# Moving the node products of a graph layer into its edge loop, and rearranging the node stage

## The chip, the cores and the metric

One core of one Trainium2 chip runs the whole kernel. The metric is the device time of one execution in microseconds (us). Five engines work side by side: TensorE (PE, whose weight loads the profile lists as PEld), VectorE (DVE), ScalarE (ACT), GpSimd (POOL) and SyncE (SP, which issues most transfers).

## The reference

A graph layer over 3125 nodes and 50000 edges sorted by target, followed by a mixture of eight experts, two per node. Both are residual.

```python
x_i, x_j = x[tgt], x[src]                       # x normalised per node, 256 features
h   = relu(concat([x_i, x_j - x_i]) @ W1 + b1)  # 512 hidden
msg = h @ W2 + b2
out = segment_sum(msg, tgt) / (deg + 1e-8)
x = x + out
xn = (layernorm(layernorm(x))) * gamma + beta
top_vals, top_idx = top_k(xn @ Wr + br, 2);  w = softmax(top_vals)
y_e = gelu(xn @ W1[e] + b1[e]) @ W2[e] + b2[e]
x = x + sum over the two chosen e of y_e * w_e
```

The kernel uses that the sum over edges can be taken before the product with W2: it sums the hidden rows of a node first and multiplies the sum.

## The kernel before, in words

Nodes are cut in 25 tiles of 128. The targets are skewed, so tile 0 has 81 blocks of 128 edges and tile 21 has 9; in all 403 blocks are filled of the 408 slots that the loop runs over.

**Preparation.** Every tile is normalised and multiplied by the lower half of W1, and the result `q` goes to memory. DVE works out where each node tile's edges start (`find_tiles`, line 594). It also sets `unsorted`, which sends the kernel into a slow general mode with up to 25 passes where the input does not fit the schedule.

**Edge loop** (lines 958 to 1531), written out as a list of steps, one for each slot. For a slot POOL gathers 128 rows of `q` (L997, 256 KB, a ring of 16 buffers). ACT copies them into a PSUM bank ("seed", L1210). PE adds the target's own part with two products (L1368, L1369). ACT rounds the relu (`h_hi`, L1226), DVE takes the rest (`h_lo`, L1054), and PE adds both into the node tile's sum (L1426, L1427). Five PSUM banks, `z_bank`, are taken in turn by the steps, and seed k waits until DVE is done with step k - 5. PE counts edges for every fourth slot (L1358). Where a node tile is complete, ACT copies its sum to `agg_all` and clears the bank (`close`, L1243 and L1250).

After every fourth slot up to slot 187 there is a "half" step: PE computes half of a tile's own part (`half_product`, L1402, and a filling product over the rest of the bank, L1373) and DVE stores it (L1076, L1098). Three more half steps for W2, after slots 207, 211 and 215, turn it and multiply it with the router's weights. SP reloads x and loads W2 in the loop (L968, L987), between the small loads that DVE's one-hot tiles wait for (L374, L1047).

**Node stage** (lines 1574 on). For each of the 25 tiles PE turns the sum (L1906, four transposes), ACT copies it (L1871), PE multiplies it with W2 and with W2 times the router's weights, 264 columns (L1913, eight instructions), POOL makes the bias (L1855) and adds it to x (L1858). DVE forms the router's part (L1640) and the residual (L1643), then statistics (L1648, L1652). ACT takes the root (L1875), DVE the inverse (L1656) and the negative mean (L1660), and ACT writes the normalised tile (L1880). SP stores x (L1580) and the normalised tile (L1584), 128 KB each, and after each third tile it loads one expert's weights (L1587, L1588, 512 KB each). All of this goes through one queue of SP. The normalised tiles live in a ring of four buffers (`XT_RING`), so that tile t can be written when the store of tile t - 4 has landed.

The expert choice runs in three parts of 16 DVE steps (`decide`): tiles 0 to 9 and 10 to 17 are interleaved with the tiles, 18 to 24 come last. When the last part is done (`s_diff`), PE computes ranks (L1926, L1927) after `AWAKE[0]` filling products (L365), then come `AWAKE[1]` more, then 100 products that list each expert's tokens (L1934), and from this list POOL starts the token gathers (L1571). The expert stage has 56 slots and is bound by PE.

Of the kernel before, what the change touches and what calls it, by code (L numbers as in the profile page):

```python
# [28 lines left out]
P = 128  # L29
EPS = 1e-5  # L30
# [6 lines left out]
AWAKE = (32, 32, 14, 6)  # L37
# [4 lines left out]
NODE_TILES = 25  # L42
HALF_PERIOD = 4
W2_GAP = 5
# [5 lines left out]
XT_RING = 4  # L50

# [28 lines left out]
def build(nc, x, src, dst, g_w1, g_b1, g_w2, g_b2, gamma, beta, wr, br, f_w1, f_b1, f_w2, f_b2, out):  # L80
# [16 lines left out]
    BATCH = 5  # L97
    assert NT == NODE_TILES and NT % 2 == 1 and 2 * H == 1024 and D == 256 and f_w1.shape[2] == H and f_w2.shape[2] == D
# [18 lines left out]
    with ctx:  # L117
# [57 lines left out]
        unsorted = sb("unsorted", [P, 1], F32, edge_ctx)  # L175
        tsort = sb("tsort", [P, SC], F32, edge_ctx)
# [13 lines left out]
        soonest = whole("soonest", [P, 1], F32, a_ctx)  # L190
        too_short = whole("too_short", [P, 32], F32, a_ctx)
# [78 lines left out]
        bias_in = sb("bias_in", [P, 2, D], F32, c_ctx)  # L270
# [89 lines left out]
        s_rel = [sem(f"s_rel{k}") for k in range(REL_RING)]  # L360

# [21 lines left out]
        with nc.Block(no_gpsimd_drain=True) as block:  # L383
# [45 lines left out]
            def _(pool):  # L429
# [21 lines left out]
                for k in range(2):  # L451
                    pool.memset(pad_i[0:1, k, :], -k).then_inc(s_const, 1)
                pool.memset(tile_hot[:].bitcast(F32), 0.0).then_inc(s_bc, 1)
# [32 lines left out]
            def _(dve):  # L486
# [107 lines left out]
                def find_tiles():  # L594
# [4 lines left out]
                    then(dve.tensor_tensor(too_soon[:, 0:NT], first_ok[:, 0:NT], base[0][:, 0:NT], ALU.is_gt))  # L599
                    now()  # L600
                    then(dve.tensor_reduce(soonest[:, :], too_soon[:, READY:NT + 1], AX.X, ALU.max))
# [10 lines left out]
                    now()  # L612

# [219 lines left out]
        s_high = sem("s_high")  # L833
        s_xback = sem("s_xback")
# [5 lines left out]
        P_HALVES = PARTS * (NT - READY)  # L840
        HALVES = P_HALVES + KD + 1
        w2_turned = [x_all[:, NT - 5 + 2 * k:NT - 3 + 2 * k, :].rearrange("p a d -> p (a d)") for k in range(KD)]
        steps = []
        for j in range(NS):
            steps.append(("slot", j))
            if half_after(j) is not None and half_after(j) < HALVES:
                steps.append(("half", half_after(j)))
        step_at = {what: k for k, what in enumerate(steps)}

        def step_no(slot0, j):  # L850

            return step_at["slot", slot0 + j] if isinstance(slot0, int) else slot0 + (j + HALVES)

        rounded = [what for what in steps if what[0] == "slot" or what[1] >= P_HALVES]
# [6 lines left out]
        def z_of(slot0, j):  # L861

            return z_bank[step_no(slot0, j) % FIRST_RING if isinstance(slot0, int) else (j + NS_ALL + HALVES) % Z_RING]
# [1279 lines left out]
```

## Time and profile before

| | |
|---|---|
| median of 3 runs | 902.34 us (899.70 to 903.33) |
| the profiled execution | 904.58 us, span 902.8 us |
| busy share of the span | PE 94%, PEld 75%, DVE 71%, ACT 71%, POOL 67% |
| edge loop, first gather to last sum | 64.5 to about 593 us |
| node stage, from its first transposes to the ranks | 595.3 to 660.7 us |
| lists of tokens | 660.7 to 681.9 us |
| expert stage | from there to the end |

Engines and lines are named as in the text above. A matmul's end is modelled and overlaps the next one, so the distance from start to start is what one costs where PE is full.

### The profile page before, as it was taken

What the parts mean: (1) busy time and instruction counts of PE and PEld (TensorE: products, weight loads), DVE (VectorE), ACT (ScalarE), POOL (GpSimd) and SP (SyncE); (2) the same over time, 40 slices, a digit from 0 to 9 for tenths busy, and PEclk for the clock granted to TensorE, in tenths of its full rate; (3) what the DMA queues carried; (4) which work ended last, traced back from release to release, by engine and by line L of the source; (5) the groups of instructions that cost most, each with busy time, mean ns of one, the idle gap of its engine ahead of it and who ended that gap; (6) DMA issues with size and microseconds to landing.
All of it is one profiled execution on the core that took longest, in us unless ns stands there. A gap on an engine that the chain in (4) does not pass through costs nothing. (4 is left out here: it accounts for less than half of the span.)

```text
span 902.8 us, 16689 instructions
## 1 busy us (share of the span) xinstructions
PE 850.4 (94%) x4164; PEld 675.2 (75%) x4165; DVE 642.3 (71%) x1762; ACT 641.3 (71%) x1398; POOL 602.9 (67%) x615
## 2 busy tenths in 40 slices
PE   9988999999999889988989888889999999999997
PEld 5446888877887668655656666668888999999996
DVE  6847898988998778877768778646894454455553
ACT  4426888888898789988989899835554555555553
POOL 2327777777777777777777777559304677776864
PEclk9998999999999989999999999999999999999999
DMA  8557877787787887887777787729852344443544
GB/s 254 174 160 225 258 240 240 240 246 244 241 238 241 240 265 233 240 248 242 241 238 238 228 240 228 208 54 279 267 134 55 60 72 72 77 78 61 83 67 49
DMA packets 90974, 169.24 MB, mean 187 GB/s; under 512 B 17608, under 2 KB 56910, under 8 KB 90840
## 3 DMA queue, kind: packets, MB, share of 16 engines
q0 software_dynamic: 43696, 122.35, 49.8%
q1 hardware_dynamic: 46232, 44.79, 16.6%
q10 hardware_dynamic: 944, 0.92, 0.4%
q8 instruction: 42, 0.69, 0.3%
q14 instruction: 60, 0.49, 0.2%
HBM read 146.98 MB, written 21.43 MB: 187 GB/s over the span
## 5 line engine op out<-in xcount | busy, mean ns | idle before, releaser
L997 POOL DMA_INDIRECT gath<-q_rows,idx_t x408 | 391.5, 960 | 137.1 <-issue 88.8
L1054 DVE SCALAR_TENSOR_TENSOR h_lo<-bank,h_hi 128x512 fp32r<-128x512 f32 x366 | 244.6, 685 | 58.5 <-ACT h_hi L1226 55.6
L1226 ACT ACTIVATE h_hi<-bank 128x512 fp32r<-128x512 f32 x366 | 216.0, 595 | 35.4 <-PE bank L1369 18.9
L1210 ACT ACTIVATE bank<-gath 128x512 f32<-128x512 f32 x366 | 219.8, 603 | 22.5 <-DMA gath<-q_rows,idx_t 17.1
L1368 PE MATMUL bank<-p_hi,ohT 128*128 x366 | 154.6, 422 | 29.9 <-ACT bank L1210 22.9
L1426 PE MATMUL agg_ps<-h_hi,oh 128*128 128x512 f32 x408 | 164.7, 404 | 2.7 <-DVE h_lo L1054 2.7
L1427 PE MATMUL agg_ps<-h_lo,oh 128*128 128x512 f32 x408 | 164.0, 402 | 0.0
L1369 PE MATMUL bank<-p_lo,ohT 128*128 x366 | 146.1, 399 | 0.0
L1368 PEld LDWEIGHTS bank<-p_hi,ohT 128*128 128x128 f32 x366 | 70.2, 192 | 74.1 <-issue 60.0
L1989 POOL DMA_INDIRECT out<-y_out,sca_i x56 | 91.7, 1637 | 40.3 <-issue 16.5
L2093 PE MATMUL bank<-tokT,fw_now 128*128 128x128 f32 x896 | 109.3, 275 | 0.8 <-ACT tokT L2049 0.8
L2059 ACT ACTIVATE actT<-bank,b1T 128x128 f32<-128x128 f32 x224 | 64.2, 368 | 61.4 <-PE bank L2093 61.4
L2105 PE MATMUL agg_ps<-fw,actT 128*128 x448 | 105.9, 380 | 0.1
L2093 PEld LDWEIGHTS bank<-tokT,fw_now 128*128 128x128 f32 x896 | 104.5, 192 | 1.0 <-DVE fw_now L2012 1.0
L1571 POOL DMA_INDIRECT agg_all<-xm_rows,gat_i x56 | 60.9, 1088 | 65.5 <-DVEq L1811 40.6
L1426 PEld LDWEIGHTS agg_ps<-h_hi,oh 128*128 128x128 f32 x408 | 78.5, 192 | 23.7 <-issue 4.6
L1040 DVE TENSOR_SCALAR oh<-iota_row,rel_t 128x128 fp32r<-128x128 f32 x408 | 91.5, 302 | 2.4 <-issue 2.4
L2032 DVE TENSOR_TENSOR y_out<-agg_ps,b2f 128x256 f32<-128x256 f32 x56 | 23.8, 425 | 95.7 <-PE agg_ps L2105 77.7
L1427 PEld LDWEIGHTS agg_ps<-h_lo,oh 128*128 128x128 f32 x408 | 78.6, 193 | 15.2
L2105 PEld LDWEIGHTS agg_ps<-fw,actT 128*128 128x128 f32 x448 | 80.9, 190 | 9.0 <-issue 0.3
L1369 PEld LDWEIGHTS bank<-p_lo,ohT 128*128 128x128 f32 x366 | 70.6, 193 | 13.0
L2049 ACT ACTIVATE tokT<-bank,gain_T 128x128 f32<-128x128 f32 x112 | 45.2, 454 | 38.9 <-PE bank L2083 38.9
(279 smaller groups left out, 1117.6 us busy)
## 6 DMA issues: line engine op xcount, KB each, us to landing
rows_sb<-rel_blocks SPq DMA_DIRECT2D x102, 128.0 KB, 4.3
fw<-in_L_ffn_W SPq DMA_DIRECT2D x16, 512.0 KB, 5.2
gath<-q_rows,idx_t POOLq DMA_INDIRECT x408, 4.3
q_rows<-q_buf SPq DMA_DIRECT2D x25, 256.0 KB, 2.8
out<-x_all SPq DMA_DIRECT2D x28, 128.0 KB, 4.0
x_all<-in_x SPq DMA_DIRECT2D x25, 128.0 KB, 2.4
xm_rows<-xt SPq DMA_DIRECT2D x25, 128.0 KB, 3.6
x_all<-in_x SPq DMA_DIRECT2D x2, 640.0 KB, 10.8
```

Of the source, the lines that this page charges most:

```text
L997: pool.indirect_dma_start(out=gath[:, j % RING, :], out_offset=None, in_=q_rows[:, :], in_offset=bass.IndirectOffsetOnAxis(ap=idx_t[:, j:j ...
L1040: ins = dve.tensor_scalar(oh[:, q % 4, k, :], iota_row[:], rel_t[:, bass.ds(local + k, 1)], None, ALU.is_equal)
L1054: dve.scalar_tensor_tensor(out=h_lo[:, j % LO_RING, :], in0=z_of(slot0, j), scalar=0.0, in1=h_hi[:, j % HI_RING, :].bitcast(F32), op0=ALU. ...
L1210: actv.activation(z_of(slot0, j), gath[:, j % RING, :], ACT.Copy).then_inc(s_seed, 1)
L1226: actv.activation(h_hi[:, j % HI_RING, :], z_of(slot0, j), ACT.Relu).then_inc(s_hi, 1)
L1368: pe.matmul(z, w, p_hi[:, tile, :], start=False, stop=True, skip_group_check=True)
L1369: pe.matmul(z, w, p_lo[:, tile, :], start=False, stop=True, skip_group_check=True).then_inc(s_exp, 1)
L1426: pe.matmul(agg_ps[:, par, :], w, h_hi[:, j % HI_RING, :], **more)
L1427: pe.matmul(agg_ps[:, par, :], w, h_lo[:, j % LO_RING, :], **more).then_inc(s_sum, 1)
L1989: pool.indirect_dma_start(out=out[:, :], out_offset=bass.IndirectOffsetOnAxis(ap=sca_i[:, i:i + 1], axis=0), in_=y_out[:, i % OUTS, :], in ...
L2093: ins = pe.matmul(bank[i % 2][:, h * P:(h + 1) * P], fw1_now[:, i % 2, k, h * P:(h + 1) * P], tokT[:, i % 2, k * P:(k + 1) * P], start=(k ...
L2105: ins = pe.matmul(agg_ps[:, i % 2, 0:D], actT[:, i % 2, k * P:(k + 1) * P], fw2[:, experts[i], k, :], start=(k == 0), stop=(k == KH - 1))
```

## The change

- 22 node tiles (`IN_LOOP`) are turned and multiplied inside the edge loop: a "turn" step after slot 211 + 9t and a "product" step after slot 217 + 9t. Each takes a bank of the ring. DVE stores the results with a predicated copy; the predicate `in_order` is false only in the slow general mode. The turned sum replaces `p_lo` of that tile, and the product replaces the sum in `agg_all`.
- Three tiles remain in the node stage, each with a bank of its own.
- The half steps for W2 come after slots 199, 203 and 207.
- Preparation compares the end of each tile with the slot by which it has to be closed, and sets `unsorted` where it is late.
- The bias is made by ACT, in a ring of four, up to nine tiles ahead; POOL only adds.
- The 22 tiles' router parts are formed by two operations. Their residual reads the product from SBUF. Root, inverse and negative mean are taken for groups of 3 or 4 tiles (`ROOTS`).
- The stores of the normalised tiles come six tiles behind those of x. `AWAKE[0]` goes from 32 to 112.

```diff
-AWAKE = (32, 32, 14, 6)
+AWAKE = (112, 32, 14, 6)
+IN_LOOP, NODE_AT, NODE_EVERY, PRODUCT_AFTER = 22, 211, 9, 6
-W2_GAP = 5
+W2_GAP = 2
+BIASES, BIAS_AHEAD = 4, 9
+        for kind, at in (("turn", NODE_AT), ("product", NODE_AT + PRODUCT_AFTER)):
+            if j >= at and (j - at) % NODE_EVERY == 0 and (j - at) // NODE_EVERY < IN_LOOP:
+                steps.append((kind, (j - at) // NODE_EVERY))
...
+    then(dve.tensor_tensor(too_late[:, 0:IN_LOOP], base[0][:, 1:IN_LOOP + 1], last_ok[:, 0:IN_LOOP], ALU.is_gt))
+    then(dve.tensor_reduce(latest[:, :], too_late[:, 0:IN_LOOP], AX.X, ALU.max))
+    then(dve.tensor_tensor(unsorted[:], unsorted[:], latest[:, :], ALU.max))
+    then(dve.tensor_scalar(in_order[:], unsorted[:], 0.0, None, ALU.is_equal))
...
+                def keep_node(kind, t):
+                    full = z_bank[step_at[kind, t] % FIRST_RING]
+                    if kind == "turn":
+                        dve.wait_ge(s_node_ps, 2 * t + 1)
+                        dve.copy_predicated(aggT_of(t), in_order[:].to_broadcast([P, H]), full).then_inc(s_lo, 1)
+                    else:
+                        dve.wait_ge(s_node_ps, 2 * t + 2)
+                        dve.copy_predicated(node_sum(t), in_order[:].to_broadcast([P, D + NEXP]), full[:, 0:D + NEXP]).then_inc(s_lo, 1)
...
+                def turn_node(t):
+                    at = step_at["turn", t]
+                    wait_after(pe, s_lo, at - FIRST_RING)
+                    wait_after(pe, s_seed, max(j for what, j in steps[:at] if what == "slot"))
+                    for h in range(KH):
+                        ins = pe.matmul(z_bank[at % FIRST_RING][:, h * P:(h + 1) * P], agg_all[:, t, h * P:(h + 1) * P], ident[:],
+                                        start=(h == 0), stop=True, is_transpose=True, skip_group_check=True)
+                    ins.then_inc(s_node_ps, 1)
+                def node_product(t):
+                    wait_after(pe, s_lo, max(at - FIRST_RING, step_at["turn", t]))
+                    for k in range(KH):
+                        pe.matmul(full[:, 0:D + NEXP], aggT_of(t)[:, k * P:(k + 1) * P], w2g[:, k, :],
+                                  start=(k == 0), stop=(k == KH - 1), skip_group_check=True)
+                    rest(full, D + NEXP).then_inc(s_node_ps, 1)
...
+        ROOTS = (0, 3, 6, 10, 14, 18, 22, NT)
+        late_bank = [agg_ps[:, 0, :], agg_ps[:, 1, :], bank7[:]]
                 for t in range(NT):
                     store_x1(t)
-                    if t:
-                        store_xt(t - 1)
+                    if t >= XT_LAG:                  # XT_LAG = 6
+                        store_xt(t - XT_LAG)
                     if t % 3 == 2 and t // 3 < NEXP:
                         load_expert(t // 3)
...
                 def residual(t):
-                    dve.wait_ge(s_gnn, t + 1)
-                    dve.scalar_tensor_tensor(out=logit[:, t, :], in0=agg_ps[:, t % 2, D:D + NEXP], ...)
+                    y = agg_all[:, t, :]
+                    if t >= IN_LOOP:
+                        y = late_bank[t - IN_LOOP]
+                        ...
                     dve.wait_ge(s_res, t + 1)
-                    dve.scalar_tensor_tensor(out=x_all[:, t, :], in0=agg_ps[:, t % 2, 0:D], scalar=rdeg[:, t:t + 1],
+                    dve.scalar_tensor_tensor(out=x_all[:, t, :], in0=y[:, 0:D], scalar=rdeg[:, t:t + 1],
                                              in1=x_all[:, t, :], op0=ALU.mult, op1=ALU.add).then_inc(s_x1, 1)
...
-                for i in range(NT + 1):
+                for i in range(NT + 4):
                     if i < NT:
                         residual(i)
+                    for b in range(len(ROOTS) - 1):
+                        if i == ROOTS[b + 1] + 2:
+                            invert(b)
                     if 0 <= i - 1 < NT:
-                        invert(i - 1)
+                        statistics(i - 1)
...
-                        pool.tensor_scalar(bias_in[:, t % 2, :], b2g, degr[:, t:t + 1], None, ALU.mult).then_inc(s_bias_in, 1)
+                def bias(t):
+                        wait_count(actv, s_res, t + 1 - BIASES)
+                        actv.activation(bias_in[:, t % BIASES, :], b2g, ACT.Copy, scale=degr[:, t:t + 1]).then_inc(s_bias_in, 1)
...
+                for b in range(len(ROOTS) - 1):
+                    root(b)
+                    for t in range(ROOTS[b], ROOTS[b + 1]):
+                        bias(t + BIAS_AHEAD)
+                        normalise(t)
```

## Rows read from the trace of the kernel before

**Rows 1.** Busy time of the engines in three stretches (PE, PEld, DVE, ACT, POOL, clock, DMA share, GB/s):

```profile
200.00:240.00 40.00, 39.71 (x178) 32.30 (x177) 36.20 (x93) 35.17 (x67) 30.24 (x33) 1.00 0.79 243
440.00:480.00 40.00, 34.17 (x131) 24.45 (x131) 30.43 (x72) 35.54 (x69) 30.54 (x32) 0.96 0.79 235
620.00:640.00 20.00, 19.98 (x105) 16.65 (x104) 16.02 (x67) 10.93 (x26) 18.88 (x24) 1.00 0.94 276
```

**Rows 2.** The gathers' line: duration min/median/max, first and last start:

```profile
L997 POOL DMA_INDIRECT gath<-q_rows,idx_t x408: 945/949/1206, 64.5 to 579.2; - x136
```

**Rows 3.** Gathers (L997) from 60 us to a time; count in brackets:

```profile
60.00:340.00 280.00, 209.01 (x219) 0.98 0.79 240
60.00:560.00 500.00, 376.10 (x392) 0.98 0.79 239
```

**Rows 4.** The same for the sums of the slots (L1427; PE and PEld):

```profile
60.00:340.00 280.00, 82.09 (x206) 39.22 (x206) 0.98 0.79 240
60.00:420.00 360.00, 108.28 (x273) 51.81 (x273) 0.98 0.79 240
60.00:560.00 500.00, 152.60 (x383) 73.22 (x383) 0.98 0.79 239
```

**Rows 5.** PE in time order around one half step (start, length, line):

```profile
201.41 1.03 PE L1402 MATMUL deg_ps<-w_wide,x_all 128*128 128x256 f32 x4
202.08 0.46 PE L1373 MATMUL deg_ps<-zero_r 128*128 128x256 f32 x1
202.38 0.39 PE L1358 MATMUL deg_ps<-oh,group_hot 128*102 128x512 f32 x1
```

**Rows 6.** PE in time order, one tile of the node stage:

```profile
626.45 0.60 PE L1906 MATMUL bank<-ident,agg_all 128*128 128x128 f32 x4
626.89 1.95 PE L1913 MATMUL agg_ps<-w_wide,aggT 128*128 128x264 f32 x8
628.67 0.60 PE L1906 MATMUL bank<-ident,agg_all 128*128 128x128 f32 x4
```

**Rows 7.** Waits from 300 to 330 us, the longest of DVE:

```profile
DVE ohT L1047 <- DMA rows_sb<-rel_blocks: 5.7, 1, 5.7
```

**Rows 8.** PE's granted clock in two stretches there (busy, clock, DMA share, GB/s):

```profile
317.00:318.00 1.00, 0.71 (x2) 0.64 1.01 340
...
324.00:325.00 1.00, 1.00 (x5) 0.95 0.57 107
```

**Rows 9.** The node stage's first transposes and SP's first store:

```profile
595.25 1.07 PE L1906 MATMUL bank<-ident,agg_all 128*128 128x128 f32 x8 [0.43 <-PEq L958]
...
599.69 2.17 SPq L1580 DMA_DIRECT2D out<-x_all  x2
```

**Rows 10.** DVE in time order, one tile of the node stage:

```profile
651.72 0.47 DVE L1643 SCALAR_TENSOR_TENSOR x_all<-agg_ps,rdeg,x_all 128x256 f32<-128x256 f32 x1
652.11 0.15 DVE L1656 RECIPROCAL rstd<-std 128x1 f32<-128x1 f32 x1
652.22 0.43 DVE L1648 BATCH_NORM_STATS2 stats<-x_all 128x6 f32<-128x256 f32 x1
...
652.78 0.19 DVE L1706 TENSOR_TENSOR score<-score,top 128x64 f32<-128x64 f32 x1
```

**Rows 11.** A POOL addition and a small DVE operation beside it:

```profile
601.85 0.73 POOL L1858 TENSOR_TENSOR x_all<-x_all,bias_in 128x256 f32<-128x256 f32 x1
601.87 0.72 DVE L1660 SCALAR_TENSOR_TENSOR nmr<-mv,rstd 128x1 f32<-128x1 f32 x1
```

**Rows 12.** DMA in a full stretch of the node stage (clock, share, GB/s):

```profile
629.00:632.00 3.00, 1.00 1.07 373
```

**Rows 13.** End of the choice: filling products, last part's first step, ranks' weight loads:

```profile
653.33 7.24 PEld L365 LDWEIGHTS deg_ps<-ident_r 128*128 128x128 f32 x32
...
656.02 0.17 DVE L1669 TENSOR_TENSOR top<-mv 128x7 f32<-128x7 f32 x1
...
660.68 0.34 PEld L1926 LDWEIGHTS bank<-pick_e,ones_mat 128*128 128x128 f32 x2
```

More of the change, by code:

```diff
@@ L97, in build, with closed_before @@
     BATCH = 5
+    P_HALVES = PARTS * (NT - READY)
+    HALVES = P_HALVES + KD + 1
+    steps = []
+    for j in range(NS):
+        steps.append(("slot", j))
+        if half_after(j) is not None and half_after(j) < HALVES:
+            steps.append(("half", half_after(j)))
+        for kind, at in (("turn", NODE_AT), ("product", NODE_AT + PRODUCT_AFTER)):
+            if j >= at and (j - at) % NODE_EVERY == 0 and (j - at) // NODE_EVERY < IN_LOOP:
+                steps.append((kind, (j - at) // NODE_EVERY))
+    step_at = {what: k for k, what in enumerate(steps)}
+    EXTRA = len(steps) - NS
+    def closed_before(t):
+        at = step_at["turn", t]
+        seeded = max(k for k in range(at) if steps[k][0] == "slot") - FIRST_SEED_AHEAD
+        return max(j for j in range(GROUP - 1, NS, GROUP) if step_at["slot", j] < seeded) + 1
+    LAST_OK = min(closed_before(t) - NODE_EVERY * t for t in range(IN_LOOP))
     assert NT == NODE_TILES and NT % 2 == 1 and 2 * H == 1024 and D == 256 and f_w1.shape[2] == H and f_w2.shape[2] == D
@@ L838, in build @@
         z_bank = [bank[0][:], bank[1][:], bank7[:], deg_ps[:, 1, :], bank[2][:]]
-        P_HALVES = PARTS * (NT - READY)
-        HALVES = P_HALVES + KD + 1
         w2_turned = [x_all[:, NT - 5 + 2 * k:NT - 3 + 2 * k, :].rearrange("p a d -> p (a d)") for k in range(KD)]
[L843 to L848, printed above, removed]
         def step_no(slot0, j):
-            return step_at["slot", slot0 + j] if isinstance(slot0, int) else slot0 + (j + HALVES)
-        rounded = [what for what in steps if what[0] == "slot" or what[1] >= P_HALVES]
+            return step_at["slot", slot0 + j] if isinstance(slot0, int) else slot0 + (j + EXTRA)
+        rounded = [what for what in steps if what[0] == "slot" or what[0] == "half" and what[1] >= P_HALVES]
         hi_at = {what: k for k, what in enumerate(rounded)}
@@ L1292, in fill_first @@
                                 high_half(j)
-                            else:
+                            elif kind == "slot":
                                 relu_hi(0, j)
@@ L1301, in first @@
                         fill_first(k)
[L1302 to L1304 removed]
+                        if kind == "slot":
+                            close_group(j, vals)
                     def fill(slot0, j, last):
@@ L1502, in first @@
                             sum_edges(0, j, known[j], known[(j, j + GROUP - 2)[j % GROUP]] if j % GROUP < 2 else None)
-                        if k + HALF_AHEAD < len(steps) and steps[k + HALF_AHEAD][0] == "half":
-                            half_product(steps[k + HALF_AHEAD][1])
+                        ahead, m = steps[k + HALF_AHEAD] if k + HALF_AHEAD < len(steps) else ("none", 0)
+                        if ahead == "half":
+                            half_product(m)
+                        if ahead == "turn":
+                            turn_node(m)
+                        if ahead == "product":
+                            node_product(m)
                         if kind == "slot" and j % GROUP == 0:
@@ L1918, in _ @@
                 pe.wait_ge(s_w2g, 16)
-                for i in range(1, NT + 1):
-                    if i < NT:
-                        turn_agg(i)
-                    product(i - 1)
+                for r in range(1, NT - IN_LOOP + 1):
+                    if r < NT - IN_LOOP:
+                        turn_agg(r)
+                    product(r - 1)
                 stay_awake(pe, AWAKE[0])
```

160 lines of the change are left out of this document (104 added, 56 removed).

## The prediction, made before the changed kernel was run

> **What bounds the kernel now.** The chain of waits ends at once in the last transfer and says nothing, so I read the busy time by stretch first, then the waits around each change, then the order in time.
>
> In the edge loop PE is busy for 39.7 of 40 us while the half steps run and for 34.2 of 40 later, ACT for 35.5 [rows 1]. POOL's 30 of 40 looks idle, but POOL sets the pace: its 408 gathers go from 64.5 to 579.2 us, so one starts each 514.7 / 407 = 1.265 us [rows 2], or 173 in 220 us between 340 and 560, 1.272 us [rows 3]. Nine slots take 11.4 us. How far the sums lie behind the gathers says whether the rest keeps up: 219 - 206 = 13 slots at 340 us, 392 - 383 = 9 at 560 us [rows 3, 4]. The lag of 13 comes from the load of W2, which held up a small load of DVE's for 5.7 us [rows 7]; PE then ran at half clock (1.2 of 2.4 GHz) from about 317.6 to 324 us [rows 8]. Afterwards the sums made 67 slots in 80 us, 1.19 us each [rows 4]. So spare capacity repaid four slots, 4 x 1.27 = 5.1 us. Nine slots cost the machine 10.7 us and the pace allows 11.4.
>
> In the node stage PE is full: 2.22 us from one tile's transposes to the next [rows 6], and 25 x 2.22 = 55.5 us. POOL is at 18.9 of 20 us there and the DMA engines at 0.94 [rows 1]. This second number matters below. From the stage's start at 595.3 us (T) to the rank products at 660.7 us it is 65.4 us [rows 9, 13].
>
> **The edge loop after the change.** A product over 512 columns costs PE 7.24 / 32 = 0.226 us [rows 13]; I take 0.23. Nine slots hold 36 of them and 2.25 counts: 38.25 x 0.23 = 8.8 us. The change adds per nine slots the transposes, 626.45 to 626.89, 0.44 us, and the product, 626.89 to 628.67, 1.78 us [rows 6]. The filling product over 248 columns shows as 202.08 to 202.38, 0.30 us [rows 5]; part of that belongs to the product before it, since four of 256 columns cannot cost 0.67 us if eight of 264 cost 1.78. So 0.1 to 0.3 us. Sum: 11.1 to 11.3 us against 11.4. PE just fits, but the slack that repaid the four slots is gone. I charge the 5.1 us in full. PE's remaining slack could repay up to 22 x 0.3 = 6 us; against it stands that a block of 1.9 us on PE delays the sum for which ACT waits at every fourth slot. I let these cancel: **+5 us**, with +0 and +25 as ends (the latter under the rivals).
>
> DVE gets a predicated copy of 512 columns and one of 264 per nine slots, an operation that no row shows. The nearest are residuals of 256 columns at 0.39 us from start to start [rows 10], so 1.2 us for both; a second pass would double it, and a copy for which half is enough would cost 0.6. DVE is busy 30.4 of 40 us [rows 1], 8.7 of 11.4, and ends between 9.3 and 11.1. I take 1.2 and no cost: it has 1.5 us of cover left. With the high end the cover is gone, and ACT's seeds, which wait for DVE five steps back, would come late (in the rivals). No step gains a wait of its own: a turn waits for seeds that the expansion before it needs anyway, a product for a copy six slots back, and both for the bank like any step. Moving the W2 half steps eight to twelve slots forward moves 3 us of PE work into the recovery and costs nothing else, as W2 is loaded at the same place.
>
> Preparation gains four small DVE operations, under 0.25 us each by the small ones of [rows 10]. The gathers start behind the stores of q, not behind this table, so I count nothing; without that cover it is 1 us.
>
> **The node stage after the change.** PE needs 3 x 2.22 = 6.7 us and drops out. Four candidates are left, each counted from T.
>
> *DVE.* An iteration between 651.72 and 652.78 takes 1.06 us, of which the inverse is 0.11 (652.11 to 652.22) and I take the same for the negative mean: 0.84 remains for residual and statistics [rows 10]. 25 x 0.84 = 21 us. Seven groups of inverse and mean: 7 x 0.35 = 2.5. Start after degrees, router part and its two new operations: 3.3 (T to the first residual, 3.9 now, less the wait for a product). Choice, parts one and two: the last part's 16 steps and three more run from 656.02 to 660.68, 4.7 us [rows 13], so 4.3 each without the three; 8.6 for two and 4.7 for the last. Together 40 us.
>
> *POOL against DVE.* An operation on 128 x 1 values took 0.72 us instead of 0.14 and ended within 0.01 us of a POOL addition that had started 0.02 us earlier: 601.87 + 0.72 = 602.59, 601.85 + 0.73 = 602.58 [rows 11]. Both read two operands from SBUF. Today's residual reads one from PSUM and is 0.47 us beside POOL's work. In 22 tiles it now reads the product from SBUF. POOL's 25 additions need 25 x 0.73 = 18 us, inside DVE's first half, so some 15 residuals meet one and wait 0.36 us on average: +5 us, with 0 and 22 x 0.73 = 16 as ends. DVE's path is then 45 us.
>
> The Trainium skill, "SBUF — State Buffer", section "Specifications (TRN2)", states this as an exclusive lock on the port pair of VectorE and GpSimd, held for a whole instruction, for a DVE operation with two SBUF inputs against a GpSimd one that reads SBUF. It speaks against moving the product to SBUF, and the trace agrees with 0.72 against 0.14 us [rows 11].
>
> *The transfers.* They were hidden behind PE's 55 us; now they are not. SP's one queue holds x (25 tiles of 0.131 MB), normalised tiles (the same) and experts (8 of 1.05 MB). The last group's root is behind ACT's normalising of tile 21, which needs the buffer of tile 17, whose store is queued behind 24 tiles of x, 17 others and 7 experts: 24 x 0.131 + 18 x 0.131 + 7 x 1.05 = 12.85 MB. The nearest row for a full machine is 373 GB/s at a share of 1.07, or 349 per unit of share [rows 12]; the mean of the stage, 276 at 0.94 [rows 1], gives 294. I take 349, as the stretch that was filled without gaps: 36.8 us. SP's first store is at T + 4.4 [rows 9], and the engines fill only with the first expert, 1.2 us lost: the store lands at T + 42.4. Then 0.6 to normalise, 0.3 root, 0.5 inverse and mean, 4.7 last part, 0.3 in semaphores: ranks at **T + 48.8**. With 294 GB/s it is T + 56.
>
> *ACT* has 25 biases and 25 normalised tiles of 256 columns; even at 0.5 us each, like a DVE operation of that width [rows 10], that is 25 us, and POOL has 20. Both lie beside DVE.
>
> The later one decides: T + 48.8 instead of T + 65.4, **-16.6 us**.
>
> By the Trainium skill, "DMA: Bandwidth & Descriptors", section "Specifications", the fabric carries 435 GB/s and HBM 358 per core; at 435 the store would land at T + 35 and DVE would decide. That is the second rival; no row moves that much over 3 us.
>
> **PE's clock.** PE's three tiles and its 112 filling products end at T + 9 + 112 x 0.226 = T + 34.5; the ranks come at T + 49. In the loop the clock fell to half behind idle time and stayed there for about 6.4 us, 317.6 to 324 [rows 8]. So the ranks and some 12 of the next 32 filling products cost twice: 12 x 0.226 = 2.7 us less a little that DVE's own path hides. **+2.5 us** (0 to 5). The other queued transfers (3.6 MB, ten us) and the tags behind them end before the token lists do, 21 us after the ranks.
>
> **Sum.** 5 - 16.6 + 2.5 = -9.1 us. Profiled time 904.6 becomes 895.5; this execution lay 2.2 us above the median, so the forecast is **893 us**.
>
> **Rivals.**
>
> 1. *The transfers don't bind* (chance 0.22). For: loads alone reach 373 GB/s. Then DVE's 45 us decides, PE is idle for 10 us less, and the sum is 5 - 20.4 + 1 = -14: 888; if the port costs nothing, 883.
>
> 2. *The loop loses more than the stage gains* (0.22, the one with the other sign). Place: PE and ACT at slots 217 to 406. ACT may wait for each of the 22 products because it closes a group every fourth slot and is busy 35.5 of 40 us [rows 1]; the predicated copy at its high end adds to the same path. Price: the 1.1 us by which one product block exceeds a half step's 0.97 us [rows 5], which was hidden, each time: 22 x 1.1 = 24. With -14 behind it that is +10 plus nothing repaid: 912 to 915. It decides from 0.65 us per product upwards (22 x 0.65 = 14). Against: during the half steps PE was at 39.7 of 40 us and the pace held [rows 1].
>
> 3. *Transfers at 294 GB/s* (0.14): 5 - 9.4 + 3 = -1.4: 901.
>
> 4. *The general mode* (0.01): a tile that ends too late for its slot sets `unsorted`, and all is run in 25 passes. With the block counts of this input the nearest of the 22 tiles ends eight slots before its limit; so this is nearly excluded. It would multiply the loop.
>
> **How the numbers follow.** Forecast 0.41. The measurement tells 0.5%, 4.5 us, from no change: faster is below 897.8 us. Forecast and first rival lie below it nearly whole (0.58), and of the others 0.06. The third lies inside, with the edge of the second and the weak end of the forecast: 0.20. Slower: 0.16. The range reaches from the first rival with a free port (0 in the loop, 881) to the second one's beginning, 906.
>
> **What would show it.** Right: L1427's count stays 12 or more slots behind L997 to 560 us and the last sum comes 4 to 6 us later; POOL's pace is unchanged; SP's stores of the normalised tiles take over 8 us to land, ACT waits for them, and the ranks start 47 to 51 us after the stage; residuals have two lengths, near 0.47 and up to 1.2 us; L365 behind the ranks takes longer than 7.3 us. Wrong: a lag of nine slots (the loop cost nothing), or ACT idle before L1226 in each nine slots (rival 2); ranks at T + 45 with stores landing in 4 us (rival 1).

## The result, and where the time went

The changed kernel takes 914.86 us (median of 6 runs, 912.52 to 916.28) against 902.42 us for the kernel before (6 runs, 899.70 to 904.93): ratio 1.0137, 95% interval 1.0118 to 1.0156. It is slower by 1.4%; the forecast was 893 us, in a range of 881 to 906. The profiled execution took 915.1 us and has a span of 913.4, 10.6 more than the 902.8 of before.

Four marks split these 10.6 us. The node stage starts (T) with VectorE's copy of the degrees, at 595.2 us before and at 614.3 now. The rank products' weight load, the first product of the token lists and VectorE's conversion of the list follow. The marks of the changed kernel (first and last start at the end of each row):

```profile
L1728 DVE COPY deg<-deg_ps x1: 185/185/185, 614.3 to 614.3; 128x25 f32<-128x25 f32 x1
...
L2050 PEld LDWEIGHTS bank<-pick_e,ones_mat x2: 286/310/333, 669.4 to 669.5; 128*128 128x128 f32 x2
...
L2058 PE MATMUL bank<-agg_all x100: 214/275/275, 679.9 to 690.9; 128*128 128x56 f32 x100
...
L1926 DVE TENSOR_SCALAR gat_i<-bank x1: 216/216/216, 691.2 to 691.2; 128x56 int32<-128x56 f32 x1
```

| stretch | before | after | difference | forecast |
|---|---|---|---|---|
| up to T | 595.2 | 614.3 | +19.1 | +5 |
| T to the ranks | 65.4 | 55.0 | -10.4 | -16.6 |
| ranks to the first list product | 8.8 | 10.5 | +1.7 | +2.5 |
| from there to the end | 233.3 | 233.5 | +0.2 | 0 |

**The edge loop.** GpSimd's gathers last started at 579.2 us [rows 2], and now ten us later:

```profile
L1034 POOL DMA_INDIRECT gath<-q_rows,idx_t x408: 944/947/1214, 64.6 to 589.3; - x136
```

The number of gathers (first two rows) and of sums (last three) from 60 us on, in brackets, answers to [rows 3, 4]:

```profile
60.00:340.00 280.00, 208.92 (x219) 0.98 0.80 240
60.00:560.00 500.00, 368.41 (x387) 0.98 0.78 235
...
60.00:340.00 280.00, 81.94 (x206) 39.39 (x206) 0.98 0.80 240
60.00:420.00 360.00, 105.07 (x265) 50.49 (x265) 0.98 0.80 240
60.00:560.00 500.00, 145.14 (x367) 69.70 (x367) 0.98 0.78 235
```

At 340 us both kernels stand alike, 219 gathers and 206 sums. Then 161 sums follow in 220 us instead of 177: 1.366 us a slot, 12.3 us for nine, where before it was 1.243. The lag of the sums grows from 13 to 20 slots. That is all it can be: a gather waits for a seed to free one of 16 buffers, and at 560 us there are 387 gathers against 371 seeds, with the sums four slots behind the seeds. So the gathers are held back too, 168 instead of 173. The seeds (L1268):

```profile
60.00:560.00 500.00, 219.77 (x371) 0.98 0.78 235
```

The waits of that stretch (340 to 580 us; total, times, longest) say who held them:

```profile
POOL gath L1034 <- ACT bank L1268: 26.5, 59, 3.1
DVE h_lo L1091 <- ACT h_hi L1284: 23.6, 35, 2.3
DVE ohT L1084 <- PE bank L1426: 22.0, 18, 2.3
...
ACT h_hi L1284 <- PE bank L1426: 16.6, 25, 1.3
ACT h_hi L1284 <- PE deg_ps L1426: 7.5, 7, 3.0
...
DVE ohT L1084 <- PE deg_ps L1426: 5.8, 6, 2.2
```

The same waits before (340 to 560 us):

```profile
POOL gath L997 <- ACT bank L1210: 12.8, 42, 0.3
DVE ohT L1047 <- PE bank L1369: 2.3, 5, 0.7
ACT h_hi L1226 <- PE bank L1369: 1.4, 7, 0.3
```

ScalarE and VectorE now wait for TensorE's expansions (L1426), 24.1 and 27.8 us, and GpSimd for ScalarE's seeds, up to 3.1 us at a time instead of 0.3. The busy times (PE, PEld, DVE, ACT, POOL, then clock, DMA share, GB/s) answer to the second line of [rows 1]:

```profile
440.00:480.00 40.00, 37.90 (x170) 29.16 (x169) 30.76 (x73) 34.65 (x67) 28.75 (x31) 1.00 0.75 230
```

TensorE went from 34.2 to 37.9 of 40 us (and its weight loads from 24.5 to 29.2); VectorE is busy for 30.8 us instead of 30.4, ScalarE and GpSimd for less than before. A node tile's product and its filling product, in order of time (start, length):

```profile
606.56 1.94 PE L1489 MATMUL bank<-w_wide,p_lo 128*128 128x264 f32 x8
608.14 0.46 PE L1430 MATMUL bank<-zero_r 128*128 128x248 f32 x1
608.45 0.40 PE L1520 MATMUL agg_ps<-h_hi,oh 128*128 128x512 f32 x1
```

It is 1.58 us and 0.31, where I had 1.78 and 0.1 to 0.3.

**The node stage.** The end of the path to the ranks, ScalarE first, then VectorE (in brackets the idle time before, and what ended it):

```profile
662.07 1.98 ACT L1993 ACTIVATE xt<-x_all,nmr,rstd 128x256 f32<-128x256 f32 x3 [2.87 <-DMA xm_rows<-xt]
663.96 0.28 ACT L1988 ACTIVATE std<-mv,eps_col 128x3 f32<-128x3 f32 x1
...
664.35 0.18 DVE L1770 RECIPROCAL rstd<-std 128x3 f32<-128x3 f32 x1 [3.64 <-ACT std L1988]
```

This is the chain of the forecast: a store of normalised rows lands at 662.1 us, T + 47.8, three tiles are normalised, the last group's root follows, and VectorE, idle for 3.6 us, makes the last choice. In the stage ScalarE waits 21.6 us for such stores:

```profile
ACT xt L1993 <- DMA xm_rows<-xt: 21.6, 7, 4.6
```

The DMA engines in two stretches of it (columns as in [rows 1]), where [rows 12] had 373 GB/s:

```profile
624.00:628.00 4.00, 4.00 (x19) 3.32 (x18) 3.97 (x16) 3.34 (x9) 4.00 (x6) 1.00 1.07 383
...
648.00:652.00 4.00, 0.35 (x2) 0.00 (x0) 0.77 (x5) 1.40 (x4) 0.49 (x2) 1.00 1.03 276
```

Both are full, and move 383 and 276 GB/s. TensorE, idle from 648 us, is granted half its clock when the ranks come: 0.53 as the mean of 652 to 674 us.

```profile
652.00:674.00 22.00, 4.64 (x10) 0.53 0.80 247
```

### The profile page after: what moved, and what is told of

Its sections match the earlier page's. It is cut to its first block and busy times, and to the rows that moved or that the text cites. A ratio compares the mean times of both kernels' runs of the same rounds, so it can differ in the third digit from the quotient of the medians.

```text
span 913.4 us, 16847 instructions
## 1 busy us (share of the span) xinstructions
PE 857.6 (94%) x4266; PEld 690.6 (76%) x4267; DVE 656.5 (72%) x1754; ACT 638.6 (70%) x1383; POOL 578.7 (63%) x591
## 5 line engine op out<-in xcount | busy, mean ns | idle before, releaser
L1091 DVE SCALAR_TENSOR_TENSOR h_lo<-bank,h_hi 128x512 fp32r<-128x512 f32 x363 | 239.5, 681 | 37.8 <-ACT h_hi L1284 35.7
L1284 ACT ACTIVATE h_hi<-bank 128x512 fp32r<-128x512 f32 x363 | 213.4, 595 | 46.4 <-PE bank L1426 32.5
L1268 ACT ACTIVATE bank<-gath 128x512 f32<-128x512 f32 x363 | 215.7, 601 | 21.8 <-DMA gath<-q_rows,idx_t 10.7
L1425 PE MATMUL bank<-p_hi,ohT 128*128 x363 | 149.9, 413 | 15.9 <-ACT bank L1268 12.4
L1520 PE MATMUL agg_ps<-h_hi,oh 128*128 128x512 f32 x408 | 161.3, 395 | 0.1
L1521 PE MATMUL agg_ps<-h_lo,oh 128*128 128x512 f32 x408 | 161.2, 395 | 0.0
L1426 PE MATMUL bank<-p_lo,ohT 128*128 x363 | 143.5, 395 | 0.0
L2113 POOL DMA_INDIRECT out<-y_out,sca_i x56 | 92.0, 1643 | 41.7 <-issue 16.5
L1084 DVE TENSOR_SCALAR ohT<-rows_sb,slot_no 128x512 fp32r<-128x512 bf16 x102 | 53.6, 526 | 44.6 <-PE bank L1426 34.2
L1426 PEld LDWEIGHTS bank<-p_lo,ohT 128*128 128x128 f32 x363 | 68.9, 190 | 12.2
## 6 DMA issues: line engine op xcount, KB each, us to landing
x_all<-in_x SPq DMA_DIRECT2D x2, 640.0 KB, 10.8
```

Source lines behind the costliest of these rows:

```text
L1091: dve.scalar_tensor_tensor(out=h_lo[:, j % LO_RING, :], in0=z_of(slot0, j), scalar=0.0, in1=h_hi[:, j % HI_RING, :].bitcast(F32), op0=ALU. ...
L1268: actv.activation(z_of(slot0, j), gath[:, j % RING, :], ACT.Copy).then_inc(s_seed, 1)
L1284: actv.activation(h_hi[:, j % HI_RING, :], z_of(slot0, j), ACT.Relu).then_inc(s_hi, 1)
L1425: pe.matmul(z, w, p_hi[:, tile, :], start=False, stop=True, skip_group_check=True)
L1426: pe.matmul(z, w, p_lo[:, tile, :], start=False, stop=True, skip_group_check=True).then_inc(s_exp, 1)
L1520: pe.matmul(agg_ps[:, par, :], w, h_hi[:, j % HI_RING, :], **more)
```

## The experiments

T and the ranks' start are read as above in each, from one profiled execution. Three kernels with the same edge loop (the changed one and the two below that move weights) have T at 614.3, 613.3 and 614.5 us; so I read a difference of 2 us, and no less.

**A first group on a disturbed chip.** Four kernels ran where even the kernel before took 1041.37 us, with stalls of 2 to 5 us on all engines all through the loop: without the product 1041.74 us, with predicated copies of 8 columns 1046.41, with both kinds of step empty 1048.80, and with the product in two pieces 1054.82. Nothing is concluded from them. Two of their questions were asked again. The two that were not leave most of the results unstored. The edit of the first, for the turned sum; the product's copy is cut in the same way:

```
-  dve.copy_predicated(aggT_of(t), in_order[:].to_broadcast([P, H]), full)
+  dve.copy_predicated(aggT_of(t)[:, 0:8], in_order[:].to_broadcast([P, 8]), full[:, 0:8])
...
```

> The changed kernel with both predicated copies cut to 8 columns (the turned sums and the products are not stored, apart from 8 columns). VectorE loses about 0.9 us of work per nine slots. Theory (PE's block): the node stage starts at 610 to 614 us. Rival (VectorE's copies): 596 to 601 us.

The other one has the small copies, and of turn and product only the filling product.

> The changed kernel with its 44 further steps left in the ring of banks but nearly empty: PE issues one filling product over a few columns in each, VectorE copies 8 columns (nothing is turned or multiplied). Theory (PE's block): the node stage starts at 595 to 597 us, as before the change. Rival (a step of the ring costs by itself, because a seed waits for VectorE five steps back and five steps now hold fewer slots): 603 to 610 us.

**Without the product.** The product's four matmuls per node tile are left out and its filling product stays, so the node sums are not multiplied by W2.

```
-  for k in range(KH):
-      pe.matmul(full[:, 0:D + NEXP], aggT_of(t)[:, k * P:(k + 1) * P], w2g[:, k, :], ...)
   rest(full, D + NEXP).then_inc(s_node_ps, 1)
```

> The product's eight instructions left out in each of the 22 product steps, once more. Theory (PE's block): the node stage starts at 596 to 599 us. Rival (VectorE's copies): above 610. Rival (further steps in the ring): above 608.

898.17 us (before on that chip 902.66), T at 597.4:

```profile
L1725 DVE COPY deg<-deg_ps x1: 184/184/184, 597.4 to 597.4; 128x25 f32<-128x25 f32 x1
...
440.00:480.00 40.00, 36.02 (x152) 27.34 (x153) 33.06 (x76) 35.77 (x69) 30.25 (x33) 0.96 0.81 244
```

So 16.9 of the 19.1 us come with the product. Transposes, filling products, both predicated copies and the 44 ring steps, all still there, cost 2.2. Whether copies or steps cost more beside the product than without it was not run on an undisturbed chip.

**The product in two pieces**, in two successive slots: the same work, half the block that sums and expansions wait behind.

```
-  for k in range(KH):
+  for k in range(piece * (KH // PIECES), (piece + 1) * (KH // PIECES)):
...
-  if ahead == "product":
-      node_product(m)
+  for piece in range(PIECES):
+      later = k + HALF_AHEAD - piece
+      if later < len(steps) and steps[later][0] == "product":
+          node_product(steps[later][1], piece)
```

> The whole computation of the changed kernel, a node tile's product issued in two pieces one step apart, once more, because in the first job every kernel, the one before the change too (1041 us), ran with stalls of 2 to 5 us on all engines all through the loop. Theory (ScalarE waits out the length of PE's block): the node stage starts at 602 to 608 us against 614.3, total 905 to 909. Rival (PE has too much work): 612 to 616 us, total 914.

912.23 us, T at 612.6. Halving the block brings 1.7 us, no more than can be read here, where half of 19 was expected. The block's length was the mechanism of my second rival, and it falls; the amount of work stands.

**The order on VectorE.** The transposed one-hot, whose waits for TensorE are new, is built behind the low part.

```
-  if j % GROUP == 2 and j // GROUP + 2 < NG:
-      build_ohT(j // GROUP + 2)
   split_lo(0, j)
+  if j % GROUP == 2 and j // GROUP + 2 < NG:
+      build_ohT(j // GROUP + 2)
```

> The changed kernel, but VectorE builds the next transposed one-hot after the low part of its slot instead of before it. In the changed kernel VectorE waits 28 us there for TensorE's expansions (2.3 us in the kernel before), with the low part that TensorE's sums want queued behind. If this order makes the loop slower, the node stage starts at least 6 us earlier than 614.3 us and the time falls to about 908. If TensorE is simply full, that wait is only where it shows: the node stage starts within 1.5 us of 614.3 and the time is 913 to 915.

911.88 us, T at 611.4. The waits there fall from 27.8 to 6.5 us, and T by 2.9: between the two answers, nearer to the second. Most of a wait of 28 us was a place where the loss shows, not its cause.

**Two and three of the four matmuls**, `range(KH // 2)` and `range(KH - 1)` in the product, whose sums are then incomplete.

> The changed kernel with two of the four matmuls of each of the 22 products left out (its output is not the reference's). With all four the node stage starts at 614.3 us, with none at 597.4. If every microsecond of the product counts once TensorE has no slack, the start lies half way, 605 to 607, and the time is about 906. If there is slack that the first half still fits into (my forecast's picture with a smaller margin), the start is below 601 and the time about 901.

> The changed kernel with one of the four matmuls of each of the 22 products left out (its output is not the reference's). The node stage started at 597.4 us without the product, at 600.6 with two of the matmuls and at 614.3 with all four. A bound that is crossed, after which each further matmul costs its whole time on TensorE (22 x 0.31 = 6.8 us), puts the start with three at 607 to 608. A cost that only the fourth brings would leave it at 601 to 602.

902.73 us and T at 600.6 with two, 904.77 and 604.3 with three. The gathers and sums of the one with two, then of the one with three (the last start, and the counts to 560 us):

```profile
L1034 POOL DMA_INDIRECT gath<-q_rows,idx_t x408: 946/947/1196, 65.0 to 578.0; - x136
...
60.00:560.00 500.00, 375.41 (x393) 0.99 0.80 240
...
60.00:560.00 500.00, 148.13 (x377) 71.27 (x377) 0.99 0.80 240
```

```profile
L1034 POOL DMA_INDIRECT gath<-q_rows,idx_t x408: 946/947/1202, 64.3 to 579.7; - x136
...
60.00:560.00 500.00, 376.29 (x393) 0.99 0.80 239
...
60.00:560.00 500.00, 147.42 (x374) 70.85 (x374) 0.99 0.80 239
```

| matmuls | T | step | last gather | lag at 560 us | PE busy, 440 to 480 us |
|---|---|---|---|---|---|
| none | 597.4 | | 579.5 | 392 - 380 = 12 | 36.0 |
| two | 600.6 | +3.2 | 578.0 | 16 | 36.7 |
| three | 604.3 | +3.7 | 579.7 | 19 | 37.5 |
| four | 614.3 | +10.0 | 589.3 | 387 - 367 = 20 | 37.9 |

One matmul is two records, a quarter of 1.58 us, so 22 x 0.395 = 8.7 us of TensorE's time over the loop. (The 0.31 in my expectation was the filling product's.) The first two, 17.4 us of work, cost 3.2 us together, the third 3.7 and the fourth 10.0, by T. My 607 to 608 for three was too late, and 601 to 602 too early.

T overstates the difference between the third and the fourth. At 300 us, before the first turned tile, the run with three already stood at 179 sums, the one with two at 177 and the one with four at 178, and a slot is worth 1.27 us. The sums of 340 to 560 us alone, without, then with two, three and four matmuls:

```profile
340.00:560.00 220.00, 69.98 (x176) 33.51 (x176) 0.98 0.80 238
340.00:560.00 220.00, 67.65 (x173) 32.54 (x173) 1.00 0.80 239
340.00:560.00 220.00, 65.84 (x168) 31.54 (x168) 1.00 0.81 237
340.00:560.00 220.00, 63.19 (x161) 30.31 (x161) 0.99 0.76 229
```

The first two matmuls cost 3 sums together, the third 5, the fourth 7. One matmul is 19 x 0.395 = 7.5 us of work in that stretch, 5.9 slots. So the first two are mostly hidden, and from the third on each costs about its own time, within the slot or so by which such counts vary (the two kernels that move weights have 162). In the forecast's own prices nine slots hold 10.3, 10.7 and 11.1 us of work with two, three and four, and take 11.4 (the gathers' pace), 11.8 and 12.3. With three and four that is 91 and 90%: as far as this estimate goes, TensorE's limit in this stretch, which the run with two matmuls just meets.

With up to three matmuls the gathers keep their pace and only the lag grows, which is paid once, at the end. With four the lag is at its limit and a late sum delays a gather: of the 19.1 us, 10.1 are the last gather's delay (579.2 to 589.3) and 9.0 the longer lag.

**Weights last.** Of the changed kernel, all 16 loads of experts' weights go behind the last store of normalised rows on SP's queue.

```
-  if t % 3 == 2 and t // 3 < NEXP:
-      load_expert(t // 3)
...
   for t in range(NT - XT_LAG, NT):
       store_xt(t)
+  for e in range(NEXP):
+      load_expert(e)
```

> The changed kernel with the 16 loads of the experts' weights (8.4 MB) issued after the last store of normalised rows instead of between the stores. If transfers hold the node stage, the stores of rows land in 2 to 3 us, ScalarE's 21.6 us of waits for them go below 5, and the ranks come 45 to 48 us after the stage starts instead of 55: 905 to 908 in all. If something else holds it (VectorE's statistics beside GpSimd's additions), the ranks stay at 53 to 55 us and the time at 913 to 915. A cost that could eat the gain: weights that land after the token lists are ready, which would show as TensorE waiting for expert weights in the block after.

912.71 us (4 runs; ratio to before 1.0108, 1.0072 to 1.0144), T at 613.3, ranks at 657.5: 44.2 us instead of 55.0, with 1.9 us instead of 5.4 for a store to land. So transfers held the stage, as forecast, and VectorE's 45 us come out behind them. The end moved by only 2.5 us (span 910.9), for another reason than I had listed: the tags' store is queued behind the weights on SP.

```profile
666.84 1.82 SPq L1691 DMA_DIRECT2D fw<-in_L_ffn_W  x1
...
669.38 2.72 SPq L1691 DMA_DIRECT2D fw<-in_L_ffn_W  x1
...
679.92 0.47 SPq L1708 DMA_DIRECT2D xm_rows<-tags  x1
```

```profile
POOL agg_all L1673 <- DMA xm_rows<-tags: 43.0, 1, 43.0
```

With a full queue even the issuing of one load takes up to 2.7 us, the tags leave at 679.9 us (675.5 as changed), and GpSimd waits for them with the first token gather, which starts at 688.4, 9 us behind the list that was ready at 679.3.

**Half the weights behind the tags.** Four experts between the stores as changed, the other four right behind the tags' store.

```
-  if t % 3 == 2 and t // 3 < NEXP:
+  if t % 3 == 2 and t // 3 < NEXP // 2:
...
   sp.dma_start(xm_rows...[:, :, D:], tags[:, :, :]).then_inc(s_tags, 16)
+  for e in range(NEXP // 2, NEXP):
+      load_expert(e)
```

> The changed kernel with the weights of four experts (4.2 MB) loaded between the stores as before, and those of the other four issued right after the store of the tags. With all eight moved behind the last store of rows the ranks came 44.2 us after the stage began instead of 55.0, but the store of the tags queued behind them. If half the bytes leave transfers enough room and the tags are no longer behind weights, the ranks come at 44 to 47 us and most of the gain reaches the end: 904 to 907. If the weights that come later are missed by the block after them, the ranks still come early and the time stays at 911 to 914.

907.96 us (6 runs; ratio to before 1.0071, 1.0047 to 1.0094), T at 614.5, ranks at 662.2, T + 47.7:

```profile
L2052 PEld LDWEIGHTS bank<-pick_e,ones_mat x2: 288/312/337, 662.2 to 662.4; 128*128 128x128 f32 x2
```

```profile
ACT xt L1995 <- DMA xm_rows<-xt: 8.2, 3, 4.3
```

Of the 7.2 us won at the ranks 6.9 reach the median (about 6 by the ratios, as the kernel before was 1.8 us faster on this chip); tags leave at 665.4 and the first token gather at 685.0. Now the node stage takes 17.7 us less than before, and what is left of the loss is the loop's.

**Fewer tiles in the loop.** IN_LOOP 8 every 24 slots, and 10 every 19, the rest after the loop; their products go through the three banks in a ring, so that product r waits for VectorE's residual r - 3. `AWAKE[0]` is 24, and with ten tiles 28 filling matmuls stand where TensorE would wait for the first bank.

```
-  IN_LOOP, NODE_AT, NODE_EVERY, PRODUCT_AFTER = 22, 211, 9, 6
+  IN_LOOP, NODE_AT, NODE_EVERY, PRODUCT_AFTER = 8, 211, 24, 6
...
+  if r > 2:
+      pe.wait_ge(s_x1, IN_LOOP + r - 2)
```

> Eight node tiles in the loop, one every 24 slots, and 17 after it, through three PSUM banks used in a ring. TensorE needs 2.6 us a tile in the stage of before, so 17 take 44 us, less than the 55 us of the stage. If each product costs the loop its own 0.8 us, the stage starts at 597.5 + 8 x 0.8 = 604; if the loop catches up between products 24 slots apart, at 598 to 600. The ranks come 54 to 55 us later either way, since transfers set that, and the time is 904 or 899 to 900. If TensorE's tiles after all bind the new stage (the rival), ranks come 60 us or more after its start and nothing is won over 905.

> Ten node tiles in the loop, one every 19 slots, 15 after it, with 28 filling matmuls where TensorE would idle for a free bank (it idled 6.6 us there with eight in the loop, and its clock fell to 0.7), and the experts' weights as in g1. The loop should lose 2 to 3 us against the kernel before (stage at 598 to 600), the ranks should come 47 to 50 us after it (TensorE's 15 tiles at 2.6 us and the wait for a bank set that), and the time 890 to 896. If the weights' late arrival costs what the ranks gain, it is 900 or more.

> As g2, but with the experts' weights where the change has them. If transfers hold the stage, its ranks come 54 to 57 us after the start and the time is 898 to 902; if TensorE's idle stretch and low clock were what held it with eight tiles in the loop (57.6 us), they come at 50 or below, and this kernel equals g2 at 890 to 896.

Eight: 908.38 us (10 runs from 900.21 to 913.08; ratio 1.0065, 1.0033 to 1.0097), T at 600.3, ranks at T + 57.5. Ten: 910.91 us (ratio 1.0104, 1.006 to 1.0148) with half the weights late, T at 602.1; 911.18 us (1.0102, 1.0068 to 1.0136) with the weights as changed, T at 600.4; ranks 63.4 and 65.4 us behind. The loop did nearly what was expected, the stage did not, and the weights' place is nearly indifferent there. TensorE's longest wait in the stage with ten tiles and the weights as changed, and its busy time, clock and DMA figures in ten us that hold most of it:

```profile
PE agg_ps L2041 <- DVE x_all L1755: 8.7, 1, 8.7
```

```profile
616.00:626.00 10.00, 2.45 (x13) 0.75 0.34 115
```

VectorE does the tiles in their order, so the first bank comes free only behind the eleventh residual. TensorE waits, its clock falls, and its fifteen tiles at over 2.2 us each end late. I had seen that wait with eight tiles and put filling matmuls there; with ten they were over at 618 us and the wait at 627.2, and they free no bank.

**A fourth bank**, `bank[2]`, with 16 tiles in the loop (every 12 slots) and 14 (every 13), half the weights late, and the one-hot behind the low part. 60 and 50 filling matmuls stand before the first wait for a bank.

```
-  late_bank = [agg_ps[:, 0, :], agg_ps[:, 1, :], bank7[:]]
+  late_bank = [agg_ps[:, 0, :], agg_ps[:, 1, :], bank7[:], bank[2][:]]
...
+  if r > 3:
+      pe.wait_ge(s_x1, IN_LOOP + r - 3)
```

> Sixteen node tiles in the loop, one every 12 slots, nine after it through four PSUM banks, 60 filling matmuls where TensorE would idle for a free bank, the transposed one-hot built after the low part, and half of the experts' weights after the tags' store. The loop's TensorE work is that of the run with three of four matmuls (stage at 604.3 us), less 1 to 3 us for the order on VectorE: stage at 601 to 604. The ranks come 47 to 50 us later and the end 243.6 us after them, as with 22 tiles and the same order of the weights: 893 to 899. If the stage's last nine tiles wait for banks as the fifteen did (ranks 63 to 65 us after the stage began), it is 908 or more.

> As h1 with fourteen node tiles in the loop, one every 13 slots, eleven after it, and 50 filling matmuls. The loop should lose 1 to 2 us less than with sixteen, and the stage 2 to 5 us more, since two more tiles of 2.6 us on TensorE come after VectorE has read the first bank again: 895 to 901. If h2 is faster than h1, the loop is still what counts, if slower, the banks are.

905.71 us (12 runs, ratio 1.0043, 1.0024 to 1.0062) with T at 607.3 and ranks 54.6 us later; 906.43 us (1.0031, 1.0007 to 1.0055) with T at 600.7 and 55.6. Neither reaches the kernel before. Fourteen give the loop back 13.6 of its 19.1 us, and the stage's products still come in one wave. Sixteen started 3 us later than expected. By the 91% estimated above, their 14.1 us of work want 15.5 of the 15.3 us of twelve slots, while fourteen fit (15.0 in 16.5 us of thirteen slots); that would be 3 of the 6.6 us between them, and the rest isn't settled.

**The mended kernel.** All 22 tiles in the loop, the product in two pieces, the one-hot behind the low part, half the weights behind the tags.

> The changed kernel (22 tiles in the loop) with the three mendings together: the product in two pieces (stage 1.7 us earlier by itself), the transposed one-hot built after the low part (2.9 us earlier), and half of the experts' weights after the tags' store (907.96 us by itself). If they add up, the stage starts at 609.9 us, the ranks come 47.7 us later and the time is 902 to 905, level with the kernel before. If the two mendings of the loop are the same microseconds, or TensorE's bound takes them back, the stage starts at 611 to 613 and the time is 905 to 908.

> The kernel of g6 once more, on a chip where the kernel before takes its usual 902 us (g6's took 1054). If the mendings add up, the stage starts at 609.9 us, the ranks come 47.7 us later and the time is 902 to 905; if the two mendings of the loop are the same microseconds, the stage starts at 611 to 613 and the time is 905 to 908.

The first run of it fell on a disturbed chip (1061.04 us against 1053.86 for the kernel before). The second: 903.43 us against 904.46 (10 and 13 runs), ratio 1.0002, 0.9984 to 1.0019. T is 611.5, so the two mendings of the loop are largely the same microseconds (2.8 us, not 4.6, as far as 2 us can be read); ranks at T + 47.6. It is the best version with the product in the loop, and equal to the kernel before.

## Why the prediction was wrong, step by step

**The failed step is the sum for the loop: "PE just fits", charged with +5 us.** It measured +19.1. The addition itself held: 8.8 us and 1.58 + 0.31 + 0.44 of product, filling and transposes per nine slots give 11.1 us, as forecast. What failed is reading 11.1 against 11.4 as room. With four matmuls nine slots took 12.3 us: priced like this, TensorE worked for no more than 90 to 91% of the time, in the runs with three and with four matmuls alike. Free room ended with two, where TensorE was busy for 36.7 of 40 us, and the sums made 173 slots in 220 us and still kept pace with the gathers. That the half steps had run at 39.7 of 40 us with the pace held [rows 1] was my evidence against. It is true as read: the lag was 8 slots at 300 us (187 gathers, 179 sums), and the same prices give 17 x 0.23 + 0.97 = 4.9 of 5.1 us per four slots, 96%. Why TensorE did more there isn't shown. One difference stands in the trace: ScalarE closed 3 node tiles in the 160 us from 120 on, and 14 in the 220 us from 340 on (15 before); no run tests it.

**The lag.** I expected it to stay at 12 or more; it grew to 20 and then slowed the gathers, which the forecast took to be unchanged. The four slots unpaid (5.1 us) are only its beginning.

**The second rival** had the sign and the size of the loop's loss (24 us), but not the mechanism: two pieces gave 1.7 us of its 19. Its start, ScalarE idle before its high part, is in the trace (24.1 us behind L1426), without being the cause. It also paired the loss with a stage of -14, not -10.4. That the measured 914.9 lies in its 912 to 915 is luck.

**Copies and ring steps** cost, with the transposes, the 2.2 us left without the product. VectorE's order has a part beside it: the one-hot behind the low part brought 2.9 us. The predicated copies took 0.730 and 0.447 us, 1.18 together, where I took 1.2:

```profile
L1142 DVE COPY_PREDICATED p_lo<-in_order,bank x18: 716/730/740, 344.9 to 602.0; 128x512 f32<-128x512 int32 x18
...
L1145 DVE COPY_PREDICATED agg_all<-in_order,bank x17: 436/447/457, 366.6 to 610.6; 128x264 f32<-128x264 int32 x17
```

**The node stage.** The right path, at the wrong rate. SP's first store left at T + 4.4 as forecast. The last wait for a store ended at 662.1 us, T + 47.8 instead of 42.4. Over these 43.4 us the DMA engines moved 305 GB/s, where I had taken 349 from a row of three us:

```profile
DMA packets 11809, 13.25 MB, mean 305 GB/s; under 512 B 891, under 2 KB 9819, under 8 KB 11805
```

The mean of the stage before, 294, was the better guide: it was my third rival (T + 56, measured 55.0). This is 5.4 of the 6.2 us missing. In the rest, three tiles (19 to 21) were left to normalise ahead of the last root (1.9 us to its start, where I had 0.6 for one), less 0.4 gained on the steps behind it: the store waited for was that of tile 15, whose buffer tile 19 takes, and not that of tile 17. The stores took 5.4 us to land in the middle and 8.3 at most; my sign had been over 8. That transfers decide is shown by the two runs that moved weights; VectorE's T + 45 by T + 44.2 without them.

The Trainium skill ("DMA: Bandwidth & Descriptors", section "Specifications") gives 435 GB/s for the fabric. In the stage no stretch came near it: 383 GB/s is the most in the stretches above. The weights alone, with the stores of rows done, did better than there, 387 GB/s as the mean of 22 us in the run with weights last, which is also above the 358 per core that this section gives for HBM:

```profile
658.00:680.00 22.00, 22.00 (x140) 19.20 (x139) 17.56 (x39) 12.99 (x52) 0.00 (x0) 0.93 1.06 387
```

**The port.** Residuals have two lengths, as forecast: 0.44 to 1.00 us for those that read the product from SBUF, 0.47 for those that read PSUM. The longest, at 637.41 us, lies beside one of GpSimd's additions (637.39, 0.73 us); those of 630.2 to 636.3 us, where GpSimd adds nothing until 634.5, take 0.45. (What the forecast quotes of the Trainium skill's "SBUF — State Buffer" stands there in the section "🔬 SBUF: two separate sides".)

```profile
L1756 DVE SCALAR_TENSOR_TENSOR x_all<-agg_all,rdeg,x_all x22: 444/542/1000, 617.9 to 652.4; 128x256 f32<-128x256 f32 x22
L1756 DVE SCALAR_TENSOR_TENSOR x_all<-agg_ps,rdeg,x_all x2: 474/474/474, 654.2 to 655.7; 128x256 f32<-128x256 f32 x2
```

It lay beside the transfers and cost nothing here.

**The clock.** From the ranks to the first list product it took 1.7 us longer than before, where I had 2.5, with TensorE granted half its clock when the ranks came.

**Two slips in the text.** The range's low end, 881, doesn't follow from its terms: the first rival with a free port is 883 with +5 in the loop, so 878 with 0. It changes nothing for a time of 914.9. And the rival that it calls the second beside the 435 GB/s is the first of its list.

## What to carry to other kernels

Work moved into a loop with spare time on one engine costs nothing only while that engine stays clear of full in a chain of several engines: here the room ended at 36.7 of 40 us busy, or at an estimated 90 to 91% by the sum of the work's prices, and from there on more work cost about its own time. Another stretch of the same loop held its pace at 96% by the same prices, so the limit is read in the stretch that gets the work. Watch the lag between the pacing engine and the last consumer: while it grows the loss is small and paid once, at the end; when the ring of buffers is full it holds back the pace. When a stage loses its bound, take the rate of the next resource from that stage's mean and not from its best stretch, and list what the shared queue still has to carry behind the bytes that are moved.

## What was not expected of the hardware

With the queue full, SP's issue of one 512 KB load took up to 2.72 us instead of the 0.43 to 0.54 of the changed kernel, so here the queue delayed its later entries already at the issue. DMA engines at a full share (1.03 to 1.07) moved 276 to 383 GB/s with loads and stores mixed, and 387 over 22 us with loads alone (share 1.06). And moving 8.4 MB out of a stage shortened it by 10.8 us and the kernel by 2.2, since one store of 50 KB came to lie behind them; with half moved, both were near 7.
